# A sixteen-sequence transformer block on one core: from a loop over pairs of sequences to a straight program with array strips

## The reference

```python
x = x + layernorm(attn_block(layernorm(x)))
x = x + layernorm(ffn_block(layernorm(x)))
```

## Time and profile before

| | |
|---|---|
| three runs | 1987.09, 1995.51, 2044.27 us; median 1995.51 |
| profiled execution, first to last instruction (span) | 2028.0 us |
| profiled execution, own time | not listed apart from the span; the slowest run is 16 us above it |
| PE busy | 1792.6 us (88%) |
| DVE, ACT, POOL busy | 677.9, 528.3, 150.0 us |
| granted TensorE clock, mean | 0.834 |

### The profile page before, as it was taken

How to read it: one execution, slowest core, us unless ns; L and a number is a source line. 1 busy time by engine, 2 the same in 40 slices (tenths; PEclk the granted TensorE clock), 3 DMA queues, 4 the chain that set the end, 5 groups by cost and what they waited for, 6 DMA issues and landing times.

```text
span 2028.0 us, 20004 instructions
## 1 busy us (share of the span) xinstructions
PE 1792.6 (88%) x6665; PEld 926.2 (46%) x6688; DVE 677.9 (33%) x2034; ACT 528.3 (26%) x1120; POOL 150.0 (7%) x210
## 2 busy tenths in 40 slices
PE   2968999899999899889999899889998899987968
PEld 1644535454354544545454544545444553542223
DVE  5235313352033532345133431335213441316011
ACT  3112132311124223231324222241222313221212
POOL 2010002100011000200011000200002000110010
PEclk8976699965599789997999688997899879995569
DMA  4000000000000000000000000000000000000000
GB/s 157 1 6 0 1 0 6 10 3 0 0 6 1 11 1 1 7 11 1 1 6 1 11 1 0 7 11 1 0 1 7 6 0 1 6 6 0 0 0 5
DMA packets 16527, 14.86 MB, mean 7 GB/s; under 512 B 1185, under 2 KB 14753, under 8 KB 16161
## 3 DMA queue, kind: packets, MB, share of 16 engines
q1 hardware_dynamic: 16416, 13.43, 2.1%
HBM read 11.33 MB, written 2.10 MB: 7 GB/s over the span
## 4 chain that ended last, share of the span: by engine, by line
PE 77%; DVE 11%; issue 7%; ACT 3%; POOL 2%; POOLq 0%; DVEq 0%; DMA 0%; SPq 0%; ACTq 0%
PE bank L940 72%; PE bank L951 2%; PE bank L1117 1%; POOL rs L376 1%; ACT junk_a L439 1%; PE bank L1170 1%; DVE mneg L849 1%; DVE M L730 1%; DVE out_sb L683 1%; DVE nrm L690 1%; DVE bstat L671 0%; DVE cv L723 0%; ACT bnT L446 0%; DVE LM L651 0%; DVE xh L683 0%
## 5 line engine op out<-in xcount | busy, mean ns | idle before, releaser
L730 DVE TENSOR_TENSOR M<-bank,LM 128x384 f32<-128x384 f32 x256 | 142.2, 555 | 630.4 <-PE bank L940 629.9
L940 PE MATMUL bank<-relu 64*128 64x256 f32 (+1 forms) x1024 | 268.3, 388 | 19.0 <-DVE M L730 12.3
L940 PE MATMUL bank<-M,xpad 128*32 128x256 f32 (+1 forms) x1024 | 242.9, 366 | 10.4 <-DVE val L735 10.4
L940 PEld LDWEIGHTS bank<-relu 64*128 64x128 f32 x1024 | 194.6, 211 | 125.5 <-issue 77.1
L940 PE MATMUL bank<-PT,Va 128*32 128x512 f32 (+1 forms) x512 | 240.8, 579 | 7.8 <-issue 6.6
L560 ACT ACTIVATE PT<-bank 128x512 f32<-128x512 f32 x192 | 114.6, 598 | 293.9 <-PE bank L940 216.4
L940 PEld LDWEIGHTS bank<-M,xpad 128*32 128x32 f32 x1024 | 99.4, 117 | 113.2 <-issue 31.3
L446 ACT ACTIVATE relu<-bank 128x512 f32<-128x512 f32 x128 | 74.8, 603 | 284.8 <-PE bank L940 282.4
L940 PE MATMUL bank<-mask_bf,ident_bf 128*128 128x256 bf16 (+1 forms) x425 | 145.3, 342 | 0.0
L848 DVE TENSOR_REDUCE mneg<-bank 128x1 f32<-128x128 f32 x256 | 73.8, 288 | 123.8 <-PE bank L940 115.2
L940 PE MATMUL bank<-Qs,w_h 128*128 128x512 f32 x256 | 113.1, 592 | 0.0
(11 more groups left out here) (201 smaller groups left out, 1947.9 us busy)
## 6 DMA issues: line engine op xcount, KB each, us to landing
x_in<-in_x SPq DMA_DIRECT2D x8, 256.0 KB, 2.8
w_h<-in_w_h SPq DMA_DIRECT2D x2, 1024.0 KB, 8.5
x_res<-in_x SPq DMA_DIRECT2D x8, 256.0 KB, 2.7
out<-out_sb SPq DMA_DIRECT2D x8, 256.0 KB, 2.4
w<-in_w SPq DMA_DIRECT2D x3, 256.0 KB, 5.6
relu<-in_w_B SPq DMA_DIRECT2D x1, 512.0 KB, 4.9
relu<-in_w_C SPq DMA_DIRECT2D x1, 512.0 KB, 6.4
rows<-in_rows SPq DMA_DIRECT2D x1, 448.0 KB, 6.5
```

What stands on the lines that cost most here:

```text
L730: v.tensor_tensor(M[:, u % 2, :], CB[:, 0:TRI], LM[:, u // 2, :], ALU.mult).then_inc(S["masked"], 1)
L940: return p.matmul(o, lhsT, rhs, start=start, stop=True, skip_group_check=True)
```

## The change

The kernel is written anew. What it computes is the same.

- **Straight program, one sequence at a time.** No loop: 16 sequences are written out, each engine with a part order of its own for the whole program (`ORDERS`). A product streams 256 columns where it had 512, and about four sequences are in flight (sequence 12 has its first part on PE when 8 has not had its last).
- **One pool of eight banks.** `BANKS` names the bank of each part; `claim` waits until the one that held it before has been read.
- **float32r in three parts** now also for the input projection, `w_1`, `w_2` and both hidden layers: 180 records of 256 columns a sequence (12 input, 48 B and C, 24 gated, 96 hidden). ACT writes the high parts, DVE or POOL the low parts.
- **Array strips.** `cb` makes the scan scores of two heads side by side, in rows 0 to 63 and 64 to 127, two banks. `v_` takes four heads, one in each column quadrant. `s_` takes four key heads, one in each strip of 32 rows, in float32r (the bfloat16 copies and their transposes are gone), four banks; its causal mask is 16 bfloat16 products of 32 columns by 32 rows. `e_` likewise, the row maximum now coming from 32-row products of `MT` by `pick`. `pv` puts four key heads in the four column quadrants.
- **GpSimd** zeroes what the transposed scores have above the diagonal (`sel`, 12 AFFINE_SELECT a sequence, after the exponential) where PE had the mask product; it has `glo`, `hlo`, the gate product `gp` and three residual sums more, and eight inverse powers a sequence where it had eight a pair.
- DVE takes the maxima 512 columns at a time (`mx`, 12 a sequence), and the decay product two heads at a time (`m`, 768 columns in two instructions, 8 a sequence).

One key head and one part of it at a time, now four. The diff, cut to the parts spoken of:

```diff
-PAIRS = BATCH // 2
...
+HEADS = (0, 2, 4, 6, 1, 3, 5, 7, 8, 10, 12, 14, 9, 11, 13, 15)
...
-    def pipeline(engine, eng, parts, first={}):
-        depth = max(ahead for _, ahead, _ in BODY[engine])
-        for i in range(-depth, 0):
-            run(engine, parts, i, False, first)
-        with eng.Fori(0, PAIRS - depth) as i:
-            run(engine, parts, i, True)
-        for i in range(PAIRS - depth, PAIRS):
-            run(engine, parts, i, False)
...
+    def run(engine, parts):
+        for name, i, k in ORDER[engine]:
+            parts[name](i, k)
...
+        def claim(name, i, k=0):
+            for last in BEFORE[name, i, k]:
+                if last is not None:
+                    pe.wait_ge(S[last[0]], at(*last))
+            return [pool8[:, b, :] for b in HOME[name, i, k]]
...
-        def scores(i, u):
-            h, s = u // 2, u % 2
-            hp, r, q0 = h // 2, (h % 2) * NS, s * L
...
-            pe.wait_ge(S["masked"], at(i, "masked", u))
-            B_, C_ = BT[r:r + NS, hp % 2, :], CT[r:r + NS, hp % 2, :]
-            mm(CB[:, 0:L], B_[:, q0:q0 + P], C_[:, q0:q0 + L], True)
-            mm(CB[:, L:TRI], B_[:, q0 + P:q0 + L], C_[:, q0 + P:q0 + L], False).then_inc(S["cb_full"], 1)
...
-        def values(i, u):
-            h, s = u // 2, u % 2
-            q0 = s * L
...
-            pe.wait_ge(S["masked"], at(i, "masked", u + 1))
-            quad = slice(32 * (h // 2 % 4), 32 * (h // 2 % 4) + 32)
-            mm(YACC[quad, q0:q0 + L], xpad[:, 2 * s, h, :], M[:, u % 2, 0:L], start=(u % 4 == 0))
-            mm(YACC[quad, q0 + P:q0 + L], xpad[:, 2 * s + 1, h, :], M[:, u % 2, L:TRI], False).then_inc(S["y_mm"], 1)
...
-        def score(i, u):
-            s, h = u // HA, u % HA
-            n, j, g, q0 = K_S + u, h // G, h % G, s * L
-            rows_ = slice(32 * j, 32 * j + 24)
-            o = ring(BACK, n)
...
-            mm(o[:, 0:P], QTb[rows_, g, q0:q0 + P], KTb[rows_, q0:q0 + P], True)
-            mm(o[:, P:TRI], QTb[rows_, g, q0 + P:q0 + L], KTb[rows_, q0:q0 + L], False)
-            mm(tri(o[:, 0:TRI]), ident_bf[:], mask_bf[:, 0, 0:2, :], False).then_inc(S["bk_full"], 1)
...
-        def weights_T(i, e):
-            s, j, c = e // EXPS, e % EXPS // 3, e % 3
-            n, q0, rows_ = K_EXP(e), s * L, slice(32 * j, 32 * j + 26)
-            o = ring(BACK, n)[:]
...
-            if c < 2:
-                o3 = o.rearrange("p (g q) -> p g q", g=2)
-                mm(o3, KT[rows_, q0:q0 + P], QT[rows_, 2 * c:2 * c + 2, q0:q0 + L], True)
-                mm(o3[:, :, 0:P], ident_bf[:], mask_bf[:, 1, 0:2, :], False).then_inc(S["bk_full"], 1)
-            else:
-                o3 = o.rearrange("p (g q) -> p g q", g=G)
-                mm(o3, KT[rows_, q0 + P:q0 + L], QT[rows_, :, q0 + P:q0 + L], True)
-                mm(o3, ident_bf[:], mask_bf[:, 1, :, :], False).then_inc(S["bk_full"], 1)
...
+        def split_product(o, w, c, x_hi, x_lo, start):
+            mm(o, w[0][:, c:c + P], x_hi, start)
+            mm(o, w[0][:, c:c + P], x_lo, False)
+            return mm(o, w[1][:, c:c + P], x_hi, False)
...
+        def bc(i, k):
...
+            pe.wait_ge(S["xnlo"], at("xnlo", i))
+            o, = claim("bc", i, k)
+            split_product(o[:, 0:L], w_B, k * P, xnH[:, 0:L], xnL[:, 0:L], True)
+            split_product(o[:, L:], w_C, k * P, xnH[:, 0:L], xnL[:, 0:L], False).then_inc(S["bc"], 1)
...
+        def cb(i, k):
+            x = BC[:, (i * 8 + k) % NBC, :]
+            pe.wait_ge(S["bcx"], at("bcx", i, k))
+            o = claim("cb", i, k)
+            for s in range(2):
+                B_, C_ = x[s * NS:(s + 1) * NS, 0:L], x[s * NS:(s + 1) * NS, L:]
+                mm(o[s][:, 0:L], B_[:, 0:P], C_, True)
+            for s in range(2):
+                B_, C_ = x[s * NS:(s + 1) * NS, 0:L], x[s * NS:(s + 1) * NS, L:]
+                last = mm(o[s][:, L:3 * P], B_[:, P:L], C_[:, P:L], False)
+            last.then_inc(S["cb"], 1)
...
+        def v_(i, q):
+            pe.wait_ge(S["m"], at("m", i, 2 * q + 1))
+            if q == 0:
+                pe.wait_ge(S["xp"], at("xp", i))
+                claim("v", i)
+            o, first = halves(bank("v", i)), q == 0
+            group = HEADS[4 * q:4 * q + 4]
+            for t_ in range(T):
+                for u, h in enumerate(group):
+                    b, e = h // 8, h % 8
+                    y = o[32 * (e // 2):32 * (e // 2) + 32, b, :]
+                    Mh_ = M[:, (i * 8 + 2 * q + u // 2) % NM, u % 2, :]
+                    if t_ == 0:
+                        last = mm(y, xpad[:, b, 0, e, :], Mh_[:, 0:L], first)
+                    else:
+                        last = mm(y[:, P:], xpad[:, b, 1, e, :], Mh_[:, L:3 * P], False)
+            last.then_inc(S["v"], 1)
...
+        def s_(i, x):
...
+            pe.wait_ge(S["ktc"], at("ktc", i))
+            pe.wait_ge(S["qtc"], at("qtc", i, 0 if x == 0 else 1))
+            o = claim("s", i, x)
+            strip = [slice(32 * j, 32 * j + 32) for j in range(HKV)]
+            heads_ = (0, 1, 2, 3) if x == 0 else (2 * x - 2, 2 * x - 1)
+            n = P if x == 0 else L
+            q0 = 0 if x == 0 else P
+            for u, g in enumerate(heads_):
+                for j in range(HKV):
+                    mm(o[j][:, u * n:(u + 1) * n], QT[strip[j], g, q0:q0 + P], KT[strip[j], 0:n], u == 0)
+            for r in range(4):
+                for j in range(HKV):
+                    c = q0 + 32 * r
+                    last = mm(o[j].rearrange("p (g q) -> p g q", q=n)[:, :, c:c + 32], mask_bf[strip[j], r, :],
+                              ident_bf[strip[j], strip[j]].unsqueeze(1).to_broadcast([32, 512 // n, 32]), False)
+            last.then_inc(S["s"], 1)
...
+        def e_(i, c):
+            pe.wait_ge(S["mtc"], at("mtc", i))
+            o = claim("e", i, c)
+            strip = [slice(32 * j, 32 * j + 32) for j in range(HKV)]
+            for j in range(HKV):
+                o3 = o[j].rearrange("p (g q) -> p g q", g=2 if c < 2 else G)
+                if c < 2:
+                    mm(o3, KT[strip[j], 0:P], QT[strip[j], 2 * c:2 * c + 2, :], True)
+                else:
+                    mm(o3, KT[strip[j], P:L], QT[strip[j], :, P:L], True)
+            for u in range(2 if c < 2 else G):
+                for j in range(HKV):
+                    g = 2 * c + u if c < 2 else u
+                    n = L if c < 2 else P
+                    last = mm(o[j][:, u * n:(u + 1) * n], PICK(strip[j], g), MT[strip[j], L - n:], False)
+            last.then_inc(S["e"], 1)
...
+        def PICK(rows_, g):
+            return pick[rows_, g:g + 1].to_broadcast([32, P])
...
+        def pv(i, c):
+            n = i * 12 + c * 4
+            pe.wait_ge(S["sel"], at("sel", i, c * 4 + 3))
+            if c == 0:
+                pe.wait_ge(S["vv"], at("vv", i))
+                claim("pv", i)
+            o = halves(bank("pv", i))
+            for u in range(2 if c < 2 else G):
+                for j in range(HKV):
+                    y = o[32 * j:32 * j + 32]
+                    w = PT[:, (n + j) % NPT, :]
+                    if c < 2:
+                        last = mm(y[:, c, :], Va[:, 0, j, u, :], w[:, u * L:(u + 1) * L], c == 0 and u == 0)
+                    else:
+                        last = mm(y[:, u // 2, P:], Va[:, 1, j, u % 2, :], w[:, u * P:(u + 1) * P], False)
+            last.then_inc(S["pv"], 1)
...
+        def hidden(name, w, i, n, ready):
+            o, = claim(name, i, n)
+            for half_ in range(2):
+                pe.wait_ge(S[ready], at(ready, i, half_))
                 for b in range(2):
+                    for k in (2 * half_, 2 * half_ + 1):
+                        c = k * HID + (2 * n + b) * P
+                        last = split_product(o[:, b * L:(b + 1) * L], w, c, gH[:, k, :], gL[:, k, :], b == 0 and k == 0)
+            last.then_inc(S[name], 1)
...
+        def sel(i, k):
+            c, n = k // 4, i * 12 + k
+            pool.wait_ge(S["ex"], at("ex", i, k))
+            w = PT[:, n % NPT, :]
+            if c < 2:
+                w = w.rearrange("p (g q) -> p g q", g=2)[:, :, 0:P]
+            else:
+                w = w.rearrange("p (g q) -> p g q", g=G)
+            g.affine_select(w, w, pattern=[[0, w.shape[1]], [1, P]], compare_op=ALU.is_ge, fill=0.0, base=0,
+                            channel_multiplier=-1).then_inc(S["sel"], 1)
```

More of the change, by code:

```diff
@@ L1281 @@
+    quarter = _np.concatenate([_np.where(r % 32 + 32 * n > c, -1e30, 0.0) for n in range(4)], axis=1)
+    tens["c_mask0"], tens["c_mask1"] = quarter[:, :L], quarter[:, L:]
+    tens["c_pick"] = _np.stack([(_np.arange(P) % 32) // 2 == g for g in range(G)], axis=1)
     inv = 1.0 / _np.float32(10000.0) ** (_np.arange(0, PA, 2, dtype=_np.float32) / PA)
[L1282 to L1283 removed]
```

1917 lines of the change are left out of this document (1012 added, 905 removed), and 83 rows, old and new, of tables (Activation, DVE, PE).

## The result

The changed kernel takes **1011.08 us** (median of 4 runs, 1008.72 to 1013.05) against 2019.89 us of the kernel before (median of 4 runs, 1987.09 to 2075.09): ratio 0.508, 95% interval 0.505 to 0.511. Ratios here are formed from the faster executions alone (1987.09 and 1995.51 us of the kernel before), since this kernel also has slower ones, at a lower granted clock. The forecast of 1260 was 249 us too high and the range ended at 1120, so the direction was right and the size wrong. Both mechanisms the forecast built on, strips side by side and float32r in one pass, are there near the forecast prices. What was off is the clock and the idle time.

A forecast was written before the change was run, and what follows sets the result against it. The prediction took PE (TensorE), 88% busy, as the bound. PE work of 57 us a sequence over clock 0.87 gives 65.5, plus 7 idle, times 16, plus 95 for the ends: 1255, forecast 1260 us, range 1120 to 1510.

The forecast's parts named there:

- Prices: PE's unit costs at the full clock, start to start, summed to 57 us a sequence where there were 92.
- the rest: PE's remaining work per sequence, said to stay: 14.4 us, bfloat16 transposes going and those of the maxima coming.
- The way back from strips: On PE, 16 changes a sequence back to the whole array, about 0.1 each; with waits that end late 2.6 us.
- Rival 1: On PE, records start strictly in program order, so strips run one record late: 1380 us, chance 0.12.
- The clock: PE's mean granted clock, taken as 0.87 after 0.834, ends 0.70 and 0.95; 57 / 0.87 = 65.5 us a sequence.
- Idle time in the middle: PE's waits between first and last sequences: 7 us a sequence, ends 4 and 14, against 11 before.
- the ends: PE's extra time at start and finish: 39 idle, 35 for the first sequence, 21 for the last, together 95 us.
- Rivals 3 to 7: 3: clock stays low, mean 0.70, 1510 us, chance 0.09; 6: 256-column float32r costs plain float32, 2210, 0.05; 7: order waits, 0.04.
- Number 4: Another engine becomes the bound, such as POOL if a `sel` takes over 3.6 us: 1600 us, chance 0.05.
- rival 5: Array strips on PE do not overlap at all, 29 us more a sequence: 1790 us, chance 0.02.

The follow-up runs named there:

- The stages: A separate kernel where TensorE alone runs product shapes one behind the other between full-array stretches; clock 0.50 with 32 and 24 rows, never falling with 32 columns or 64 rows.

## Why the prediction was wrong, and where it was right

**Prices: right.** Per sequence, start to start less idle: 180 float32r records with the starts behind strips 24.2 us (21.6 + 2.6 forecast), `cb` 6.6 (7.2), `v` 3.2 (3.2), `pv` 3.1 (3.0), `s` 2.0 (2.6), `e` 2.2 (2.4), the rest 15.8 (14.4). That is 57.2 as it ran and, at the full clock, 55.8 where 57 was forecast. `cb` was put at 0.90 by analogy with the columns and takes 0.85, where one head alone took 0.84. For `cb`, `s_` and `e_` no row of before showed row strips side by side; the forecast chose values near the low end of wide bounds, and that they fit is the analogy borne out, not a price read. The way back from strips was read from a row that leads into `scores` (0.32 where 0.23 is the stream); it takes 0.22 where 0.12 is, the same 0.1. DVE 40 us a sequence (41), ACT 37 (34 plus table loads). POOL's 29 (31) is in part luck: the selects cost 5.7 (0.41 and 0.65 us, where the nearest rows, 0.55 and 1.04, gave 9) and the eight powers about 0.70 to 0.75 each instead of 1.01, while `gL` costs 1.29 instead of 1.04.

**Rival 1: refuted.** In `v` four first records stand within 0.1 us and `pv` takes 1.00, not 2.0; on one strip it takes 3.57. *TensorE: Matmul & The Clock Gate*, Part 3, of the Trainium skill has matmuls start and end strictly in program order. These rows disagree with it only where it is read record by record, as rival 1 did: in the earlier trace rows the second record of a product starts behind the first record of the next one, and `v` has its records in fours 0.22 apart (502.52 to 502.74), one for each strip. No row shows a product that starts before one ahead of it.

**The clock: the step that failed first.** The prediction read 0.54 over 441 to 564 as the mark of "`score` and scan units" and took 0.87, because small products stay in the program. The stages show that products shaped like the scan's (64 rows, 32 columns) do not lower it; `score` with 24 rows and `QT,KT` with 26 did, and over that stretch 0.54 became 1.00 when they read all rows. The change puts four such products side by side, 128 rows at work. What is left is 50 us at the half level, 10 of them between 120 and 900 and the rest at the two ends, and the mean is 0.975. The term: 57 / 0.87 is 65.5 a sequence, 57 / 0.975 is 58.5; times 16, **113 us** of the miss. The end of 0.95 given for the clock was too low as well.

**Idle time in the middle: the step that failed second.** Forecast 7 us a sequence, ends 4 and 14; measured 23 us in 780, 1.8 a sequence. The argument "PE's work shrinks while DVE's and ACT's does not, which makes waits likelier" carried over the kernel before, in which PE waits for 11 us of each sequence. The run with one sequence at a time shows what was underrated: the same parts leave PE idle 44% of the time alone and 3% with three to four in flight. Together with the ends (73 us, 95 forecast) the idle time is 95 instead of 207, **112 us** of the miss. The low prices (55.8 for 57) make up 20 more. The two steps are not independent: with one sequence in flight the waits took the clock to 0.691, so fewer waits are also part of why the clock is high.

**Rivals 3 to 7** did not come. Number 4 is nearest to something real: DVE has less room than its busy share says, though at 40 us of 61 it does not bind. For rival 5, all strips on one gave 1507.

What stays open: why less of the work taken from DVE comes back than goes through of the work added; no run drew up a new order for the new load. It is also open how much of the 253 us that the kernel before still spends at the half level with full rows comes from waits.

## What to carry to other kernels

Read the clock by what kind of product runs where it falls, not only by how busy PE is: here products of 24 and 26 rows, a fifth of PE's time in the stretch, went with 1.2 GHz while PE was 98% busy, and putting four of them side by side gained their overlap and the clock. A sum of unit prices, most of them read from the trace, start to start, came within 3% for a kernel in which most parts were new; the terms that were taken over from the old kernel as averages, clock and idle share, were both wrong. To bound idle time, count sequences in flight.

## What the runs showed of the hardware that was not expected

A float32r record whose weights have 32 rows and 128 columns costs 0.11 us with 128 moving columns and 0.13 with 256 (`MT,pick` on one strip), so halving the columns of such a record gains next to nothing there. And GpSimd can be held up while VectorE works. Two additions of two columns each on POOL in the head of the changed kernel:

```profile
11.89 0.20 POOL L426 TENSOR_TENSOR rin<-mv,eps_ln 128x2 f32<-128x2 f32 x1 [9.55 <-DVE mv L900]
...
20.86 3.44 POOL L436 TENSOR_TENSOR rin<-ssq,eps_rms 128x2 f32<-128x2 f32 x1 [6.46 <-ACT junk L597]
```

The same instruction takes 0.20 and 3.44 us; in the second case DVE made the low parts of the weights from two operands in SBUF, from 21.28 to 24.25. The run with the other order of the head bears it out: there this addition stands at 15.72, ahead of the low parts, and takes 0.28, and the instruction that now meets them, a product of 256 columns that took 0.72 at 24.26 in the changed kernel, takes 3.58, until 0.8 us after their end at 24.4:

```profile
21.57 3.58 POOL L464 TENSOR_TENSOR xr<-xh,rows 128x256 f32<-128x256 f32 x1 [4.68 <-DVE LM L851]
```

*GPSIMD Engine Reference*, section 1, of the Trainium skill has POOL contend for its SBUF interfaces with VectorE instructions that read two SBUF inputs; these rows agree. It is no rule that every such meeting costs: many of the additions of two columns that run beside DVE in the rest of the trace take 0.20. Nor does it explain the 1.29 of `gL`: the squares `hid` on POOL, like the earlier trace rows a product of 512 columns with itself, take 1.04 to 1.07 in the changed kernel too.
